# The last block's projections, norm and router moved between the first expert tiles; early tile table from 13 blocks; zero rows stored one region a turn

## The reference

```python
x = x + xattn(layernorm(x), ctx, Wq, bq, Wk, bk, Wv, bv, Wo, bo)    # 16 heads of 32, 154 keys
y = layernorm(x)
w = softmax(y @ W_router.T + b_router)                               # 8 experts, the two largest kept
x = x + sum_e w[e] * (y @ W_experts[e].T + b_experts[e])
```

## Time and profile before

| | before |
|---|---|
| median of 3 runs (lowest, highest) | 1371.55 us (1371.31, 1374.33) |
| the profiled execution: time, span | 1366.51 us, 1364.8 us |
| mean granted PE clock | 0.953 of full speed |
| busy: PE, PEld, DVE, ACT, POOL | 1227.5, 743.6, 860.4, 636.1, 883.1 us |

### The profile page before, as it was taken

The page is one execution under the profiler, slowest core; times in us unless marked ns, Lnnn a source line. Parts: engine busy times, 40 slices in busy tenths (PEclk is TensorE's granted clock), DMA queues, the critical chain, the costliest instruction groups (busy, mean ns, idle before and its releaser), DMA issues. The chain is left out here.

```text
span 1364.8 us, 37333 instructions
## 1 busy us (share of the span) xinstructions
PE 1227.5 (90%) x11552; PEld 743.6 (54%) x11553; DVE 860.4 (63%) x1905; ACT 636.1 (47%) x914; POOL 883.1 (65%) x1124
## 2 busy tenths in 40 slices
PE   5696899999998999899999997777899999999997
PEld 3352666665665656666566565443455555555553
DVE  3363687877787678687688676744455555555544
ACT  2204557546655645754754753512333343433333
POOL 5112467878878878878878966966544555454445
PEclk9787899999999989999999998888999999999999
DMA  8814456537647647656654655677999999899786
GB/s 238 224 35 128 116 152 193 188 119 232 200 127 226 179 137 221 173 166 191 193 181 126 209 156 164 243 278 185 245 178 171 173 175 175 167 168 179 143 160 120
DMA packets 136024, 240.07 MB, mean 176 GB/s; under 512 B 18533, under 2 KB 49509, under 8 KB 134757
## 3 DMA queue, kind: packets, MB, share of 16 engines
q1 hardware_dynamic: 102432, 160.67, 40.1%
q0 software_dynamic: 29952, 67.73, 24.4%
q10 hardware_dynamic: 3525, 10.06, 2.0%
HBM read 113.34 MB, written 101.71 MB: 158 GB/s over the span
## 5 line engine op out<-in xcount | busy, mean ns | idle before, releaser
L1778 PE MATMUL S<-we_s,wq_s 128*128 x1632 | 379.5, 383 | 13.9 <-DVE wq_s L1734 5.8
L1711 POOL DMA_INDIRECT out<-xn,to x136 | 210.6, 1549 | 210.1 <-DMA out<-xn,to 80.6
L1111 POOL TENSOR_TENSOR we_s<-P_s,we_s 128x1024 f16<-128x1024 f32 x112 | 239.3, 2155 | 51.2 <-ACT we_s L876 25.5
L1778 PEld LDWEIGHTS S<-we_s,wq_s 128*128 128x128 f16 x1632 | 159.2, 99 | 183.6 <-issue 24.7
L1722 ACT ACTIVATE wq_s<-PVp 128x512 f16<-128x512 f32 x138 | 82.1, 596 | 238.6 <-PE PVp L1768 238.3
L925 DVE TENSOR_REDUCE mx_sb<-S 128x6 f32<-128x924 f32 x160 | 170.9, 1110 | 2.1 <-PE S L684 2.1
L702 PE MATMUL W<-wo_s,aT_hi 128*128 128x512 f16 x512 | 162.7, 384 | 3.6 <-DVE xR_s L935 2.1
L667 PE MATMUL W<-we_s,wq_s 128*128 128x512 f16 x512 | 162.2, 389 | 3.2 <-DVE we_s L913 1.6
L1202 POOL DMA_INDIRECT dispatched<-xn,idx x128 | 126.6, 989 | 47.6 <-issue 46.7
L1756 DVE SCALAR_TENSOR_TENSOR att<-S,be_s 128x512 f32<-128x512 f32 x136 | 94.1, 692 | 97.9 <-PE S L1778 97.0
L768 PE MATMUL PVp<-Vr,we_s 128*128 128x132 f16 x768 | 92.9, 234 | 42.9 <-POOL we_s L1111 42.2
(11 more groups left out here) (190 smaller groups left out, 2038.0 us busy)
## 6 DMA issues: line engine op xcount, KB each, us to landing
P_s<-dispatched SPq DMA_DIRECT2D x140, 260.5 KB, 3.6
we_s<-we_s SPq DMA_DIRECT2D x192, 128.0 KB, 4.0
be_s<-in_x SPq DMA_DIRECT2D x16, 1024.0 KB, 9.7
xR_s<-in_x SPq DMA_DIRECT2D x16, 1024.0 KB, 6.1
out<-xR_s SPq DMA_DIRECT2D x16, 1024.0 KB, 10.4
wst<-in_weT SPq DMA_DIRECT2D x16, 512.0 KB, 7.5
we_scratch<-wsp SPq DMA_DIRECT2D x16, 512.0 KB, 6.9
Kst<-k_scratch SPq DMA_DIRECT2D x16, 480.0 KB, 5.7
```

The source lines that it names most:

```text
L1111: e.tensor_tensor(Pst[1][:, r:r + 2, :], exps(n), Pst[0][:, r:r + 2, :], ALU.subtract).then_inc(pldp, 1)
L1711: e.indirect_dma_start(out, bass.IndirectOffsetOnAxis(ap=to[u][:, :], axis=0), yw[u % YW], None, bounds_check=N - 1, oob_is_err=False, com ...
L1778: m = e.matmul(Yp[:, u % 2, :], gT[u % 2][xp][:, k, :], we_s[:, bass.ds(n * WN + (wp * KC + k) * D, D)], start=(c == 0), stop=(c == 11))
```

## The change

- Block 15's projection pieces 3 to 11, their reading and statistics, its norm on ACT and POOL and RQ leave the slots. PE now does pieces 3 to 5, the transposes of tiles 0 and 1, pieces 6 to 11, tile 0, the logits (`pe_LB`), tiles 1 to 5, the ranks (`pe_R`), and so on.
- On POOL the first four scatters of block 14 move out of slot 16, behind add 0, and the second four from behind add 0 to behind add 1; so do block 15's NC and RQ (behind add 2), RP (behind add 4), NA, RW, SC and SD.
- DVE does the logits' step after tile 2 (before: after tile 0), RS and RE after tile 6 (after tile 3), and the pieces of the late table after tiles 9, 10 and 11.
- EARLY is 13: the early table is made in slot 14, covers 96 tiles (TURNA = 12), and the first loads wait for 13 blocks' scatters.
- SP issues the first four tile loads, then the three expert loads, then the other loads; the store of block 15's sums (`sp_XS`) moves from behind load 7 to behind load 11; the zero rows move from between the loads 12 to 19 to one behind each of the turns 2 to 9.
- Some waits gain "or it > 0", which is needed where turn 1 is written out too.

The core of the diff (in the slot functions every step of block 15's projection, its reading and its statistics gets the same condition; one place of each kind is shown):

```diff
-EARLY = 14
+EARLY = 13
 TURNA = (TOPK * TB * EARLY // P - NE) // TU
 TILEA = TURNA * TU
...
-        if on_bm1:
+        if on_bm1 and not bm1.last:
             pe_O(e, bm1, 3, s)
             pe_O(e, bm1, 4, s)
             pe_O(e, bm1, 5, s)
...
-        if on_bm2:
+        if on_bm2 and not bm2.last:
             act_norm(e, 1, bm2)
...
-        if on_bm2:
+        if on_bm2 and not bm2.last:
             dve_SN(e, bm2, 3)
             dve_norm_var(e, 1, bm2)
...
-        if on_bm1:
+        if on_bm1 and not bm1.last:
             dve_Oe(e, bm1, 1)
             dve_SN(e, bm1, 1)
...
-        if on_bm2 and not bm2.last:
+        if on_bm2 and bm2.here(NB - 3):
             pool_SC(e, bm2)
...
-        if on_bm1:
+        if on_bm1 and not bm1.last:
             pool_NC(e, bm1, 1)
             pool_RQ(e, bm1)
-        if on_bm2 and not bm2.last and bm2.here(NB - 3):
+        if on_bm2 and bm2.here(NB - 3):
             pool_SD(e, bm2)
...
     def sp_zero_rows(e, n):
-        if n == 0:
-            e.wait_ge(zset, 2)
-            e.dma_start(xs_d[SPARE:ROWS, :], zrow).then_inc(zst, 16)
-            e.wait_ge(tbz, 1)
-        r = e.value_load(baseI[0:1, n:n + 1], min_val=0, max_val=SPARE - P)
+        r = e.value_load(baseI[0:1, bass.ds(n, 1)], min_val=0, max_val=SPARE - P)
         e.dma_start(xs_d[bass.ds(r, P), :], zrow).then_inc(zst, 16)
...
-            load_experts(e, 5, NE)
             e.wait_ge(phd, 10 * NB)
             e.wait_ge(pldp, NP * NB)
             for p in range(2):
                 for k in range(TOPK):
-                    e.wait_ge(scat[p][k], 64 * EARLY // 2)
+                    e.wait_ge(scat[p][k], 64 * ((EARLY + 1 - p) // 2))
             e.wait_ge(ld_t[0], 16)
-            for u in range(2 * XG):
+            for u in range(XG):
                 sp_load(e, 0, u)
+            load_experts(e, 5, NE)
+            sp_turn(e, 0)
             sp_XS(e, LAST)
-            for u in range(XG):
-                sp_load(e, 1, u)
-            for u in range(TU):
-                sp_load(e, 1, u + XG)
-                sp_zero_rows(e, u)
+            sp_turn(e, 1)
             load_table(e, 1)
-            turns(e, lambda it: sp_turn(e, it), 2, TURNA - 1, lambda: sp_rest_stored(e))
+            e.wait_ge(zset, 2)
+            e.dma_start(xs_d[SPARE:ROWS, :], zrow).then_inc(zst, 16)
+            e.wait_ge(tbz, 1)
+            with e.Fori(0, NE) as n:
+                sp_turn(e, n + 2)
+                sp_zero_rows(e, n)
+            turns(e, lambda it: sp_turn(e, it), 2 + NE, TURNA - 1, lambda: sp_rest_stored(e))
...
             pool_add(e, 0, 0)
+            pool_SC(e, LAST + (-1))
+            pool_add(e, 0, 1)
             pool_SD(e, LAST + (-1))
-            pool_add(e, 0, 1)
             pool_add(e, 0, 2)
+            pool_NC(e, LAST, 1)
+            pool_RQ(e, LAST)
+            pool_add(e, 0, 3)
+            pool_add(e, 0, 4)
             pool_RP(e, LAST)
-            pool_add(e, 0, 3)
+            pool_add(e, 0, 5)
             pool_NA(e, LAST, 1)
-            pool_add(e, 0, 4)
+            pool_add(e, 0, 6)
+            pool_add(e, 0, 7)
             pool_RW(e, LAST)
-            pool_add(e, 0, 5)
+            pool_add(e, 1, 0)
+            pool_add(e, 1, 1)
             pool_SC(e, LAST)
-            pool_add(e, 0, 6)
+            pool_add(e, 1, 2)
             pool_SD(e, LAST)
-            pool_add(e, 0, 7)
...
             act_hi(e, 0, 2)
+            act_norm(e, 1, LAST)
             act_weigh(e, 0, 0)
...
-                if u == 3:
+                if u == 5:
                     act_RX(e, LAST)
...
+            for j in range(1, 2):
+                dve_Oe(e, LAST, j)
+                dve_SN(e, LAST, j)
             e.wait_ge(qp, 4 * NB)
-            e.wait_ge(atp, 4 * NB)
-            e.wait_ge(ld_ew, 16 * (NE + 1))
             e.wait_ge(ld_t[0], 16)
             dve_glo(e, 0, 0)
             dve_glo(e, 0, 1)
+            for j in range(2, NJ):
+                dve_Oe(e, LAST, j)
+                dve_SN(e, LAST, j)
+            dve_norm_var(e, 1, LAST)
+            e.wait_ge(atp, 4 * NB)
+            e.wait_ge(ld_ew, 16 * (NE + 1))
             dve_tile(e, 0, 0)
+            dve_tile(e, 0, 1)
+            dve_tile(e, 0, 2)
             dve_RB(e, LAST)
             dve_RM(e, LAST)
-            for u in range(1, 4):
+            for u in range(3, 7):
                 dve_tile(e, 0, u)
             dve_RS(e, LAST)
             dve_RE(e, LAST)
-            dve_tile(e, 0, 4)
-            dve_tile(e, 0, 5)
+            dve_tile(e, 0, 7)
+            dve_tile(e, 1, 0)
             dve_RI(e, LAST)
...
+            for i in range(3, 6):
+                pe_O(e, LAST, i, LAST + (-(-1)))
             e.wait_ge(ld_t[0], 16)
+            e.wait_ge(nmd, 4 * NB)
+            pe_turn_rows(e, 0, 0)
+            pe_turn_rows(e, 0, 1)
+            for i in range(6, 12):
+                pe_O(e, LAST, i, LAST + (-(-1)))
             e.wait_ge(ld_ew, 16 * (NE + 1))
-            e.wait_ge(nmd, 4 * NB)
             e.wait_ge(exd, 10 * NB)
             if ND:
                 e.wait_ge(pldd, ND * NB)
-            pe_turn_rows(e, 0, 0)
-            pe_turn_rows(e, 0, 1)
+            pe_tile(e, 0, 0)
             pe_LB(e, LAST, LAST + (-(-1)))
-            for u in range(TU):
+            for u in range(1, TU):
                 pe_tile(e, 0, u)
-                if u == 3:
+                if u == 5:
                     pe_R(e, LAST, LAST + (-(-2)))
```

More of the change, by code:

```diff
@@ L1703, in pool_add @@
         hold(e)
-        if in_loop(it) or u > 0:
+        if in_loop(it) or it > 0 or u > 0:
             new = of_tile(e, i, 2, 16)
             for back in range(1, YW):
-                if in_loop(it) or u >= back:
+                if in_loop(it) or it > 0 or u >= back:
                     e.wait_ge(add_y[(u - back) % YW], added(it, u - back) - 16 + new)
@@ L1726, in act_weigh @@
         e.wait_ge(ye, done(i))
-        if in_loop(it) or u >= YW:
+        if in_loop(it) or it > 0 or u >= YW:
             e.wait_ge(add_y[u % YW], added(it, u - YW))
@@ L1741, in dve_weights @@
         e.wait_ge(ywd, done(i - TU))
-        if in_loop(it):
+        if in_loop(it) or it > 0:
             e.wait_ge(add_y[u % YW], added(it, u - TU))
@@ L1845, in _ @@
             pool_add(e, 0, 0)
+            pool_SC(e, LAST + (-1))
+            pool_add(e, 0, 1)
             pool_SD(e, LAST + (-1))
-            pool_add(e, 0, 1)
             pool_add(e, 0, 2)
+            pool_NC(e, LAST, 1)
+            pool_RQ(e, LAST)
+            pool_add(e, 0, 3)
+            pool_add(e, 0, 4)
             pool_RP(e, LAST)
-            pool_add(e, 0, 3)
+            pool_add(e, 0, 5)
             pool_NA(e, LAST, 1)
-            pool_add(e, 0, 4)
+            pool_add(e, 0, 6)
+            pool_add(e, 0, 7)
             pool_RW(e, LAST)
-            pool_add(e, 0, 5)
+            pool_add(e, 1, 0)
+            pool_add(e, 1, 1)
             pool_SC(e, LAST)
-            pool_add(e, 0, 6)
+            pool_add(e, 1, 2)
             pool_SD(e, LAST)
-            pool_add(e, 0, 7)
-            turns(e, lambda it: pool_turn(e, it), 1, TURNA, lambda: e.wait_ge(ld_t[1], 16))
+            for u in range(3, TU):
+                pool_add(e, 1, u)
+            turns(e, lambda it: pool_turn(e, it), 2, TURNA, lambda: e.wait_ge(ld_t[1], 16))
             for q in range(YW):
@@ L1900, in _ @@
             dve_RE(e, LAST)
-            dve_tile(e, 0, 4)
-            dve_tile(e, 0, 5)
+            dve_tile(e, 0, 7)
+            dve_tile(e, 1, 0)
             dve_RI(e, LAST)
-            dve_tile(e, 0, 6)
+            dve_tile(e, 1, 1)
             ch = table_counts(e, 1)
+            dve_tile(e, 1, 2)
             table_experts(e, 1, ch)
-            dve_tile(e, 0, 7)
+            dve_tile(e, 1, 3)
             table_rows(e, 1, ch)
-            turns(e, lambda it: dve_turn(e, it), 1, TURNA, lambda: e.wait_ge(ld_t[1], 16))
+            for u in range(4, TU):
+                dve_tile(e, 1, u)
+            turns(e, lambda it: dve_turn(e, it), 2, TURNA, lambda: e.wait_ge(ld_t[1], 16))
         @block.tensor
```

## The result

The changed kernel takes 1376.78 us in the median of 20 runs (1370.38 to 1384.5) against 1371.14 us for the kernel before (1363.65 to 1377.63): ratio 1.0047, 95% interval 1.0028 to 1.0067. It is slower by 4 to 9 us, where 1369.4 was forecast and slower had a chance of 0.26. The time lies inside the stated range, but on the slower side of no change.

A forecast was written before the change was run, and what follows sets the result against it. TensorE was taken as the bound from tile 21 on, with losses ahead of it and in the tail. Terms -0.6 + 2 + 2 - 5.5 = -2.1 us gave 1364.4 us, 1369.4 carried to the median; range 1363 to 1378.

The forecast's parts named there:

- New order of the first tiles: From attention's end to tile 21: POOL's wait eats the order's gain; tile 21 at 999.4 against 999.96, -0.6 us.
- The first loads: Tile loads' 14.8 us wait for block 13's scatter goes; costed inside the step on the first tiles' order.
- The wait ahead of tile 5: DVE's logits step needs POOL's RQ behind adds and scatters: tile 5 starts at 944.7 instead of 931.9.
- Tiles 6 to 21 nearly free of stalls: Loads held up by scatters, the 1 MB store and late adds cost only +2 us (ends 0 and +6).
- The 17 us of POOL wait eat the order's gain: First tiles: POOL's wait uses up what the new order gains, leaving tile 21 -0.6 us.
- Zero rows one a turn: Eight zero stores spread over tiles 16 to 79 cost PE 0.25 us each, +2 us (0 to 8 in all).
- rival b: Steady loop: zero stores delay the load after each, up to 1 us of PE eight times; +3.9, 1375.5 us; chance 0.20.
- The early table: Moved to slot 14, its long DVE operation waits for POOL; attention ends 3.6 us later (ends 0 and +4.6).
- The tail: Last tiles: with the table of 13 blocks the tail's loss of 5.5 us goes (ends 0 and -5.5).
- (a): Table fits slot 14 without waiting for POOL, so the 3.6 us go: -5.7, 1365.9 us; chance 0.25.
- (c): POOL's late scatters and adds stall tiles after the first expert boundary (tile 12): +2 to +4, about 1374.5 us; chance 0.15.

The follow-up runs named there:

- e10: Changed kernel with the early table of 14 blocks and the burst of zero rows put back (new order alone): 1382.66 us, ratio 1.0094 to the kernel before.
- e7: Kernel before with only the zero rows stored one region a turn, in turns 2 to 9: 1364.1 us, ratio 0.9959.
- e4: Kernel before with only the early table of 13 blocks and its scatter wait: 1365.97 us, ratio 0.9983.
- e1: Changed kernel with the early table of 14 blocks again: 1379.36 us, ratio 1.0083 to the kernel before.
- e5: Changed kernel run again, nothing edited: 1374.94 us, ratio 1.0053 to the kernel before.
- e9: Kernel before profiled a second time, nothing edited: one run, 1363.57 us.
- e3: Changed kernel with SP's three expert loads issued at the end of the slots again, ahead of the table wait: 1375.46 us, ratio 1.0059 to the kernel before.
- e6: Changed kernel with the edits of e2 and e3 together: 1358.66 us, ratio 0.9928 to the kernel before.
- e2: Changed kernel with block 14's scatters, NC and RQ ahead of add 0 on POOL: 1364.02 us, ratio 0.9964 to the kernel before.
- e12: Kernel before, in its old order, with the table of 13 blocks and zero rows one region a turn: 1358.36 us, ratio 0.9944.
- e11: e6 with the early table of 14 blocks: 1364.19 us, ratio 0.9965 to the kernel before.
- e8: e6 with block 15's eight scatters later, four after add 13 and four after add 15: 1358.62 us, ratio 0.9921 to the kernel before.

## Why the prediction was wrong, point by point

The parts, timed alone, nearly add up: the order +12.9 us (e10; the interval is 8 to 18), the spread zero rows -5.6 (e7), the table of 13 blocks -2.3 (e4), together +5.0, where +6.4 (1.0047) and +7.3 (1.0053) were measured. Inside the changed kernel the zero rows bring less (1.5 us, e10 against e1) and the table more (4 to 5, e1 against changed).

The prediction's -0.6 for the order already holds the table's +3.6 in slot 14, and it counts the burst of zero rows as gone. So it compares with the kernel that has both, e1: -0.6 - 3.6 + 2 for the order without the table, +2 for the zero stores, -0.2 us in all. Measured were +11.3. For the table it had +3.6 - 5.5 = -1.9, and that was about right. **The step that failed is "New order of the first tiles".** From the end of attention to tile 21 on PE it had 107.4 us (1001.4, with the +2, less 894.0, which is 890.38 + 3.6), 2.2 less than the 109.6 of the profile before. The changed kernel took 127.9 and 121.8 us in its two profiles (the second profile of before 114.3). In three stretches:

| from PE's first matmul of a tile to that of another | forecast | changed | e5 | before | e9 |
|---|---|---|---|---|---|
| end of attention to tile 0 | 21.3 | 28.6 | 27.5 | 24.2 | 26.7 |
| tile 0 to 6 | 37.0 | 40.3 | 40.3 | 28.4 | 29.1 |
| tile 6 to 21 | 49.1 | 59.0 | 54.0 | 57.1 | 58.5 |

- *"The first loads": a wait that goes.* It didn't. The 14.8 us for scatters became 17.0 us for the table's arrival. "I cost this inside the next step" gave no price to the three expert loads that the change puts behind this wait, although PE waits for all of them before tile 0. They were issued 14.9 us later than before, and tile 0 waited 7.42 us. That is most of the 6 to 7 us of the first row: e3, whose expert loads aren't late, starts tile 0 at 23.7. By ratios the wait is worth about 5 us once POOL's wait is gone too (e6 against e2), and nothing seen while it stands (e3).
- *The wait ahead of tile 5* was right: 12.8 us forecast, 13.67 in the profile, with RQ done at 945.85 and add 0 at 926.84, 19.0 us apart, where 940.1 and 921.1 were forecast, also 19.0 apart. e2 takes it away, and 11 to 12 us go with it. The 3.3 us more in the second row have their place ahead of that: tile 0 was to run at the full clock, with add 0 5.8 us behind its start; after its wait it ran mostly at the lower one (4.45 us), and add 0 came 8.8 us behind.
- *Tiles 6 to 21 nearly free of stalls, "+2 us".* The kernel before loses 10 us or more in this stretch, and the prediction dropped them for a reason: the burst of zero stores leaves it. For the old order that reason holds (e7: 48.1 us against 55.5 and 57.0, where 15 x 3.03 are 45.5). In the new order the stretch is as slow without the burst (57.3, 52.3 and 55.9 us in the changed kernel, e5 and e1), and the burst put back changes little (58.3, e10). "Ends 0 and +6" was too narrow. What fills it isn't shown. It isn't only POOL's wait, since the repaired order also takes 50.4 to 56.3 us. One thing that moved in is the 1 MB store, which the prediction named and did not price by itself. In e5 the load right behind it, of tile 12, took 6.6 us to land (first row, issues from 980.5 to 983 us), while those of tiles 15 to 17 took 4.4 (second row, 992 to 1003):

```profile
P_s<-dispatched SPq DMA_DIRECT2D x1, 260.5 KB, 6.6
```
```profile
P_s<-dispatched SPq DMA_DIRECT2D x3, 260.5 KB, 4.4
```

No run moves that store alone, so its share is open, as is that of the late adds.

"The 17 us of POOL wait eat the order's gain": with that wait and the one for weights gone (e6), the order gains 3.5 us up to tile 6, where projections and router steps hide behind tiles, and gives 2.8 back up to tile 21. By ratios 2.2 us are left (e6 against e12), not clear of noise. So there was little to eat.

*Zero rows one a turn.* The forecast for the steady part (+2, rival b up to +8) falls: PE waits for loads 0.2 us in it. The gain had no term of its own; it was inside the pace assumed for tiles 7 to 21. e7 gives it one, 5.6 us for the whole program in the old order.

*The early table.* Its cost in slot 14 was about right: from DVE's L985 in slot 14 (just ahead of the table's place) to RQ of block 14 the changed kernel takes 73.3 us, before 70.6: +2.8, and 3.6 were forecast. DVE's idle time of 5.44 us ahead of the RECIPROCAL at 825.64 is gone; that operation starts 7.9 us after L985 instead of 5.8, so 2.1 us late where 4.6 were forecast, since of the table's two long operations only the second waited for POOL (0.17 and 2.05 us). *The tail* was right in kind and too large: from tile 111 to the end, six profiles with a table of 14 blocks have a mean of 86.0 us and eight with 13 one of 83.1 (from the table above), 3 us less where 5.5 were forecast. Pair by pair it is 3.4 to 4.0 us (e1 against changed and e5, e7 against e12, e11 against e6), but nothing in e4 against the two profiles of before. The stalls left are shown above, 0.82 and 1.06 us ahead of the tiles at 1310.81 and 1324.15, put down to DVE's bias operation; an expert boundary still costs POOL 5.09 to 6.16 us of waiting in the tail. That the pair gains more than 3 less 2.8 lets expect (2.3 us in e4, 5 in e11) was not in the sum; in e11 part of it is seen: the loads wait 14.2 us for block 13's scatters, PE 4.44 us for the first load.

*The rivals.* (a) falls for the changed kernel: one long operation of the table did wait for POOL. In e6 and e12 they hardly did (0.39 and 0.16 us), so this turns on where the two engines stand. (b) falls by the waits for loads, though its 1375.5 us is the number nearest to the result; that is luck. (c) named the right stage and sign, but its mechanism isn't shown: e8, in the repaired order, shows no gain from moving the last block's scatters, and in the changed order nobody moved them.

The Trainium skill (SBUF — State Buffer, "SBUF: two separate sides") has VectorE wait for a GpSimd operation that holds the shared port pair. The profiles agree. In the changed kernel DVE's L1094 starts at 821.73 (shown above), after the start of POOL's pair at 821.64, and takes 2.05 us. In e6 it starts at 824.65, half a microsecond ahead of POOL's pair at 825.16, and takes 0.16 us:

```profile
821.64 4.20 POOL L1111 TENSOR_TENSOR we_s<-P_s,we_s 128x1024 f16<-128x1024 f32 x2
```
```profile
824.65 0.16 DVE L1094 TENSOR_TENSOR te<-te 128x1 f32<-128x1 f32 x1
```
```profile
825.16 4.22 POOL L1111 TENSOR_TENSOR we_s<-P_s,we_s 128x1024 f16<-128x1024 f32 x2
```

## What to carry to other kernels

Before a stall is counted as gone, ask what else moves into its stage. Here the burst of stores was the cause in the old order (e7), and the new order, without the burst, was as slow there. Where an engine's order is written by hand, a short step that others wait for (here RQ, 0.25 us) belongs ahead of the first instruction that has to wait for a late result, and bulk loads belong ahead of a wait, since a wait taken away in a queue is often replaced by the next one in it. Time each part of a bundled change alone: this one held two gains (7.7 us together, e12) and a loss of 12.9 us, and the loss hid them. Parts obtained by subtracting one bundle from the next add up by construction; only parts timed alone test the sum.

## What the runs showed of the hardware that was not expected

- A DVE operation of 0.16 us on 128 values takes 2.05 us when it starts 0.1 us after a wide POOL operation, and the wait ends with the running one of POOL's two operations, not with the pair: L1094 ends at 823.78, the pair at 825.84.
- The same attention stage ends between 883.5 and 892.1 us in 12 profiles whose instructions up to there differ by little more than the table's slot, and at 902.9 and 903.7 in the two others (e5, e8). Why isn't known.
- Eight stores of 260.5 KB inside some 28 us cost 5.6 us of the whole program though the DMA share from 960 to 1000 us was 0.99 with them and 0.96 without: the share alone doesn't tell whether the bytes are those that PE waits for. The same stores, one in eight loads, cost next to nothing: PE waits 0.2 us for loads in the steady part of the changed kernel.
- The fetch of the small table (1.1 KB), issued by ACT behind its expert loads, landed 10.0, 12.7 and 13.9 us after its issue in e5, e3 and e6, where a tile's load of 260.5 KB took 2.9 us in e5. Whether the loads ahead of it are the cause wasn't tested.
